# Cross-attention and mixture-of-experts layer: the three groups of transposed probabilities stand behind the 14th expert block instead of around it

## What is computed

```python
q, k, v = ln(x) @ Wq, ctx @ Wk, ctx @ Wv                # 8 heads of 64
x = x + softmax(q @ k.T / 8) @ v @ Wo + bo               # cross-attention, 77 keys
rw = routing weights of 16 experts from ln(x)            # softmax over the gated logits
q, k, v = [sum over experts e of rw[e] * (ln(x) @ proj[e]) for proj in (q_proj, k_proj, v_proj)]
x = x + sum over e of (rw[e] * causal_attention(q, k, v)) @ o_proj[e]
```

## Time and profile before

| | |
|---|---|
| Median of 3 runs | 2564.55 us (2564.33 to 2565.59) |
| Profiled execution | 2566.21 us, span 2564.4 us |
| Mean granted TensorE clock | 0.984 |
| Instructions | 54407 |
| TensorE matmuls | 2481.6 us busy, 97%, x17308 |
| Weight loads | 2429.9 us, 95% |
| VectorE | 2120.9 us, 83% |
| ScalarE | 1582.7 us, 62% |
| GpSimd | 1104.6 us, 43% |
| DMA | 441.48 MB, mean 172 GB/s |

### The profile page before, as it was taken

The page is one execution under the profiler, slowest core; times in us unless marked ns, Lnnn a source line. Parts: engine busy times, 40 slices in busy tenths (PEclk is TensorE's granted clock), DMA queues, the critical chain, the costliest instruction groups (busy, mean ns, idle before and its releaser), DMA issues.

```text
span 2564.4 us, 54407 instructions
## 1 busy us (share of the span) xinstructions
PE 2481.6 (97%) x17308; PEld 2429.9 (95%) x17308; DVE 2120.9 (83%) x6123; ACT 1582.7 (62%) x5126; POOL 1104.6 (43%) x1743
## 2 busy tenths in 40 slices
PE   5699999999999999999999999999999999999996
PEld 4699999999999999999999999999999999999996
DVE  5688888888888888888888888888888888888874
ACT  5566666666666666666666666666666666666642
POOL 2144444444444444444444444444444444444443
PEclk8799999999999999999999999999999999999998
DMA  5655555565555556465565556466565556555531
GB/s 169 209 183 170 185 171 178 157 191 177 177 183 177 172 175 189 147 207 172 165 202 171 167 173 196 146 203 181 166 186 176 178 155 193 173 179 175 177 101 35
DMA packets 288054, 441.48 MB, mean 172 GB/s; under 512 B 20340, under 2 KB 199476, under 8 KB 279707
## 3 DMA queue, kind: packets, MB, share of 16 engines
q1 hardware_dynamic: 218139, 369.84, 44.4%
q10 hardware_dynamic: 69632, 68.17, 10.8%
HBM read 254.86 MB, written 181.83 MB: 170 GB/s over the span
## 4 chain that ended last, share of the span: by engine, by line
PE 81%; DVE 6%; POOL 5%; issue 3%; ACT 3%; DMA 1%; SPq 0%; POOLq 0%; DVEq 0%; ACTq 0%
PE bank_b L540 12%; PE bank_b L541 12%; PE bank_b L542 12%; PE bank_c L540 5%; PE bank_c L541 5%; PE bank_c L542 5%; PE bank_a L541 4%; PE bank_a L540 4%; PE bank_a L542 4%; PE bank_a L685 3%; PE bank_a L649 2%; PE bank_a L661 2%; PE bank_a L650 1%; DVE both L1315 1%; PE bank_a L624 1%
## 5 line engine op out<-in xcount | busy, mean ns | idle before, releaser
L1423 DVE SCALAR_TENSOR_TENSOR acc<-bank_b,rw,acc 128x192 f32<-128x192 f32 x1792 | 653.4, 408 | 111.4 <-PE bank_b L542 109.0
L540 PE MATMUL bank_b<-wqkv_hi,x2T_lo 128*128 128x384 f32 (+1 forms) x2048 | 720.3, 352 | 2.4 <-ACT acc L1047 2.0
L541 PE MATMUL bank_b<-wqkv_lo,x2T_hi 128*128 128x384 f32 (+1 forms) x2048 | 693.7, 339 | 0.0
L542 PE MATMUL bank_b<-wqkv_hi,x2T_hi 128*128 128x384 f32 (+1 forms) x2048 | 690.1, 337 | 0.0
L1748 POOL TENSOR_TENSOR mixs_lo<-mix,mixs_hi 128x512 fp32r<-128x512 f32 x256 | 380.8, 1519 | 166.1 <-ACT mixs_hi L1121 166.1
L1017 ACT ACTIVATE probs<-bank_a,s_max 128x77 f32<-128x77 f32 x1024 | 317.2, 329 | 207.9 <-DVE s_max L1353 207.9
L540 PEld LDWEIGHTS bank_b<-wqkv_hi,x2T_lo 128*128 128x128 f32 x2048 | 386.4, 189 | 4.6 <-ACT acc L1047 2.4
L541 PEld LDWEIGHTS bank_b<-wqkv_lo,x2T_hi 128*128 128x128 f32 x2048 | 386.9, 189 | 0.0
L542 PEld LDWEIGHTS bank_b<-wqkv_hi,x2T_hi 128*128 128x128 f32 x2048 | 384.9, 188 | 0.0
L540 PE MATMUL bank_c<-wo_hi,mixs_lo 128*128 128x256 f32 x1024 | 288.4, 282 | 3.7 <-POOL mixs_lo L1748 3.7
L1121 ACT ACTIVATE mixs_hi<-mix 128x512 fp32r<-128x512 f32 x256 | 160.0, 633 | 206.8 <-DVE mix L1464 206.8
(11 more groups left out here) (224 smaller groups left out, 6357.4 us busy)
## 6 DMA issues: line engine op xcount, KB each, us to landing
gq<-g_dram SPq DMA_DIRECT2D x63, 1232.0 KB, 5.5
rw_all<-rw_dram ACTq DMA_DIRECT2D x128, 512.0 KB, 6.8
uo<-u_dram SPq DMA_DIRECT2D x63, 1024.0 KB
g_dram<-draft SPq DMA_DIRECT2D x105, 462.0 KB
u_dram<-draft SPq DMA_DIRECT2D x127, 308.0 KB
g_dram<-mixs_lo SPq DMA_DIRECT2D x63, 462.0 KB
xt<-in_x_dram SPq DMA_DIRECT2D x64, 256.0 KB, 4.7
out_dram<-mix SPq DMA_DIRECT2D x64, 256.0 KB, 3.9
```

The costliest lines, as they stand in the source:

```text
L540: nc.tensor.matmul(dst, lhs[1], rhs[0], start=start, stop=False)
L541: nc.tensor.matmul(dst, lhs[0], rhs[1], start=False, stop=False)
L542: return nc.tensor.matmul(dst, lhs[0], rhs[0], start=False, stop=stop)
L1423: V.scalar_tensor_tensor(acc[:, t, k, :], src, rw[:, t, e:e + 1], acc[:, t, k, :], ALU.mult, ALU.add).then_inc(b_evac, 1)
```

## The change

On TensorE and on VectorE block 13 moves ahead of the groups 0 and 1 of the transposed probabilities, so that the three groups follow one another between block 13 and block 14. ScalarE, GpSimd and the sync queue keep their order.

```diff
@@ -877,9 +877,9 @@
                 do(earlier, c_y, 3)
                 turn("E2")
                 do(before, b_qkv, 12)
+                do(before, b_qkv, 13)
                 fill("PT0", probs_of, a_pT, 0)
                 fill("PT1", probs_of, a_pT, 1)
-                do(before, b_qkv, 13)
                 fill("PT2", probs_of, a_pT, 2)
                 do(before, b_qkv, 14)
                 turn("E3")
```

## The result

The changed kernel takes 2609.76 us (median of 4 runs, 2608.58 to 2614.95) against 2564.96 us (4 runs, 2564.33 to 2565.59): the ratio is 1.0179, with a 95% interval from 1.0167 to 1.0191. It is slower, as forecast, but by 44.8 us instead of 16, and so outside the range. Spread over 62 steps that is 0.72 us a step instead of 0.26. Of all the runs in this document one stands apart, one of the ten of bcast_first: it took 4859.98 us beside 2562.5 to 2566.84 us of the other nine, nothing on record explains it, and the ratio leaves it out.

A forecast was written before the change was run, and what follows sets the result against it. TensorE's work and its waits were taken to bound the kernel. Steps longer by 0.27, 0.32 and 0.20 us, mean 0.26, times 62 steps gave 16 us on 2564.5: 2580.5 us, range 2570 to 2592 us.

The forecast's parts named there:

- TensorE: 0: Term on TensorE: same instructions in another order, ten transposes together, no switch left to save; 0 us.
- faster: Rival on TensorE: 0.09 us ahead of the transposes is a switch, one saved per step; 2559 us, chance 0.05.
- the clock: Rival on TensorE: ten transposes in a row lower the granted clock, 1.1 us a step; 2633 us, chance 0.02.
- ScalarE: the issues hold the eviction: Term on ScalarE: group 2's eviction waits behind two broadcast DMA issues and starts 0.96 us later.
- No change: Rival on ScalarE: group 2's eviction runs under the issues, so nothing shows; 2564.5 us, chance 0.17.
- The failed step: Second broadcast issue on ScalarE, 1 us later beside sync-queue issues: taken at its present length, forecast 0.26 us a step.
- VectorE and the slack: Term on VectorE: 0.55 us idle ahead of block 15 takes most of a 0.90 us delay, leaving 0.27 us.
- L722 and M2: TensorE's waits: next activations' transposes (L722) stop it for 0.43 us, context product's (M2) shrinks; step longer by 0.27 us.
- (c): At L722, block 14's bank is free late for the second pair of next activations' transposes; TensorE stops 0.43 us.
- (d): At the context product in slot M2, the old wait for E3's eviction shrinks; step grows 0.27 us, not 0.43.
- Nothing is taken back: Rival: the context product's wait in slot M2 absorbs nothing, each step pays 0.43 us; 2591 us, chance 0.13.
- Item (a): Slot E3's weight load, 0.02 us late for group 0's bank, is covered by a 384-column matmul; 0 us.

The follow-up runs named there:

- bcast_first: Changed kernel with ScalarE issuing the two routing-weight broadcasts ahead of its eviction of transposed-probabilities group 0: 2565.11 us, ratio 0.9996.
- store_later: Changed kernel with the sync queue storing slot E2's result behind slot E3's, some 5 us later: 2584.1 us, ratio 1.0072.
- E3: Not a run: a slot of each step, whose bank VectorE evicts behind block 15 and the context product waits for; no time of its own.
- vector_half: Kernel before with block 13 moved ahead of groups 0 and 1 on VectorE only, TensorE in its old order: 2577.05 us, ratio 1.0042.
- issue_apart: Changed kernel with the first broadcast issued ahead of ScalarE's eviction of group 2, the second behind it: 2577.32 us, ratio 1.0044.
- half_bcast: Changed kernel with each of the two broadcasts cut to half, four of eight expert pairs: 2606.63 us, ratio 1.0169.
- bcast_last: Kernel before with ScalarE issuing the two broadcasts behind its eviction of group 2 instead of ahead: 2582.8 us, ratio 1.0066.
- E1: Not a run: a slot of each step, whose result is stored in some kinds of step; no time of its own.

## Why the prediction was wrong in size and right in kind

**What bounds the kernel**: right. TensorE and the waits it makes set the time, before and after.

**TensorE: 0**: right. Ten transposes start at 1306.52, block 14 at 1307.53, 1.01 us for ten, and bcast_first comes out at 0.9996. So the rivals *faster* (a switch saved) and *the clock* fell: the granted clock is 1.00 in all three steps. The Trainium skill, "TensorE: Matmul & The Clock Gate", section "Part 4: PE-mode transpose", has it that a transpose does not count as busy for the clock in the same way; ten in a row, 1.01 us between matmuls, did not lower it here.

**ScalarE: the issues hold the eviction**: right, in every step (0.04 to 0.05 us from the issue's end to the eviction). *No change* fell with that. The Trainium skill's "DMA: Bandwidth & Descriptors", section "Issuing engines are not separate DMA queues", calls the sequencer's time for starting a DMA usually small relative to the DMA. It is: 1.33 us against 6.9 us. But it is time in which ScalarE starts nothing else, and ScalarE had an eviction to make.

**The failed step**: "What no row shows is how long an issue takes 1 us later, beside others of the sync queue." I took the second issue at its present 0.66 us. It takes a median of 1.53 us in kind U and 0.87 us in kind G, because a store has just been issued on the sync queue. Measured as the difference between the changed kernel and store_later, that is 25.7 us of the 44.8. And I bounded the term wrongly: I named the issue as the unknown, but gave it an upper end of 0.43 us a step, which is the price of another doubt (whether M2 takes its wait back). The earlier trace rows had a longer one: 1.04 us. At 1.04 us in every step each would have cost 0.38 us more, 62 x (0.26 + 0.38) = 40 us, 2604 us, and the range would have had to reach at least there. The longest of the whole trace before is longer still:

```profile
L1112 ACTq DMA_DIRECT2D rw_all<-rw_dram x128: 581/654/1268, 140.7 to 2526.1; - x128
```

Its 1.27 us belong to a second issue, at 141.42 in the opening, with a store of the sync queue issued 0.45 us ahead of it. At 1.27 us in every step the sum is 62 x (0.26 + 0.61) = 54 us, 2618 us, and a range up to there has the measured time in it. And the sync queue's timeline of the kernel before, which I didn't set beside ScalarE's, had E2's store in step A:

```profile
1287.67 0.73 SPq L425 DMA_DIRECT2D u_dram<-mixs_lo  x2
```

The second issue starts at 1287.66, with the store's; moved by 1.04 us it comes behind it.

**VectorE and the slack**: right. VectorE's idle time ahead of PT2's low part is 1.27 us and named ScalarE; ahead of block 15 there is none; block 14 comes at 1310.68, 21.77 us into the step. The forecast had 21.08 (1290.64 less 1269.56); the 0.69 us between them are the longer issue (1.33 - 0.66).

**L722 and M2**: right. In store_later, whose second issue is as short as I took it, the third transpose at L722 starts 0.40 us late in kind U, 0.43 in G and 0.33 in V (medians), where (c) had 0.43. In the changed kernel it is 1.26, 0.65 and 0.33 us, for the reason above. M2's wait has shrunk as in (d): its weights still follow VectorE's low part of E3 by 0.05 us, in store_later (ends at 1299.62 + 0.68) and in the changed kernel (1311.98 + 0.68) as before. From the timelines of weight loads, store_later and then the changed kernel:

```profile
1299.11 0.32 PEld L722 LDWEIGHTS bank_b<-ident,mix 128*128 128x128 f32 x2 [0.43 <-DVE acc L1423]
...
1300.35 0.19 PEld L624 LDWEIGHTS bank_a<-cT_hi,wv_lo 128*128 128x128 f32 x1
...
1312.71 0.19 PEld L624 LDWEIGHTS bank_a<-cT_hi,wv_lo 128*128 128x128 f32 x1
```

*Nothing is taken back* (2591 us) was not the case: store_later's steps are longer by 0.32, 0.31 and 0.18 us, less than L722 is late. Beyond that nothing more is taken back. VectorE has no idle time left ahead of block 15, so a longer issue moves L722's bank and E3's bank alike, and goes to the step in full (U: 0.86 us at L722, 0.85 us in the step, from store_later to the changed kernel). That is my own "each 0.1 us on the issues is 6 us", which proved right.

**Item (a)**, that a late weight load is covered, made no difference in the change, but it is wrong: in vector_half a load held up 0.27 us lengthens the step by 0.22.

## What to carry to other kernels

Before an instruction moves on an engine that also issues DMAs, treat each issue as an instruction of that engine with a length of its own, and read the other hardware queue's timeline at the new place, not only the old: here the length went by what had just been issued there. Where a price is named as unknown, its bound must be on that price, by the longest such row in the trace, here 1.27 us. And look for an engine that idles just ahead of an eviction that TensorE waits for: swapping VectorE's block 15 and slot E3 gave 17 us with two lines.

## What the runs showed of the hardware

One of the two DMA issues on ScalarE takes 0.58 to 0.66 us as a rule, and the second up to 2.35 us (the changed kernel) where the sync queue had a store issued about a microsecond earlier. From the starts in step A: with the store's issue 0.01 us later it is 0.66 us (before) or 0.65 us (vector_half, same place); 1.05 us behind the store's it is 1.33 us (the changed kernel), 1.13 us behind it 1.28 us (issue_apart), 1.05 us behind 2.10 us (half_bcast, half the bytes). The first of the two, 0.41 us behind the store's in the changed kernel and 0.83 us behind in bcast_last, stays at 0.6 us. Whether it escapes because it comes too early or because it is the first of two, no run tells; a first issue a full microsecond behind a store wasn't tried. Behind E2's store a `u` result (two DMAs) lengthens more than a `g` result (one), medians 1.53 against 0.87 us; behind E1's, in bcast_first, it does not (0.97 and 1.02 us). Nor is such a store the only cause: a single step of kind V in the changed kernel has a second issue of 1.43 us, and a single step of store_later one of 1.55 us, with no store of E2 ahead. The sync queue's own issues lengthen as well, in the kernel before from 1293.65 two of `u_dram` in 1.50 us, where the two from 1287.67 take 0.73 us.

The Trainium skill's "DMA: Bandwidth & Descriptors", section "Queues, rings and completion order", says that the sync and ScalarE queues have rings on the same 16 DMA engines and no descriptor generator of their own. The runs agree in so far as a store of the one lengthens an issue of the other; that the store from GpSimd leaves it at 0.66 us decides nothing, since its packets came later.
